# Moving on-chip tiles by multiples of 64 bytes against each other in an attention, dense and LoRA-SwiGLU kernel

## The reference

```python
x = x + attention(x, ...)      # 32 query heads, 8 key/value heads of 128, 512 cached keys + 128 new ones, RMS norm, rotation
x = x + (x @ W.T + b + (x @ sign(mask[b])) * coeff[b])
x = x + down(silu(gate(x)) * up(x))      # width 1376; gate, up and down each with a LoRA of rank 16, chosen per sequence
x = x + x @ weight[adapter_id[b]].T
```

## Time and profile before

| | us |
|---|---|
| three runs | 1366.54, 1367.86, 1368.14; median 1367.86 |
| the profiled execution, its time | 1367.71 |
| its span, first to last instruction | 1365.6 |
| TensorE busy | 1347.4 (99%) |
| VectorE busy | 1040.9 (76%) |
| ScalarE busy | 840.0 (62%) |
| GpSimd busy | 714.9 (52%) |

### The profile page before, as it was taken

One profiled execution on the slowest core, in us unless ns is written; L12 is line 12 of the kernel. 1 busy time (PEld: TensorE's weight loads), 2 busy tenths in 40 slices (PEclk: granted clock), 3 DMA queues, 4 the chain that ended last, 5 costly groups with the idle time before them and its releaser, 6 DMA issues. The chain is left out here.

```text
span 1365.6 us, 24886 instructions
## 1 busy us (share of the span) xinstructions
PE 1347.4 (99%) x7810; PEld 1189.8 (87%) x7810; DVE 1040.9 (76%) x2122; ACT 840.0 (62%) x2212; POOL 714.9 (52%) x970
## 2 busy tenths in 40 slices
PE   8999999999999999999999999999999989999998
PEld 7898898888889888899888889888888868888886
DVE  7888777877787778777877787778777877748547
ACT  7666665666566666665666666566655774545444
POOL 7766465546555655555555555564545633413204
PEclk9999999999999999999999999999999999999999
DMA  5355225522552264136414631573210453355432
GB/s 198 97 178 166 63 80 168 151 66 77 188 128 53 79 205 130 31 108 200 108 31 134 203 77 31 154 208 99 63 31 17 139 173 124 123 185 163 164 124 84
DMA packets 161994, 163.91 MB, mean 120 GB/s; under 512 B 121488, under 2 KB 129296, under 8 KB 151568
## 3 DMA queue, kind: packets, MB, share of 16 engines
q1 hardware_dynamic: 156144, 128.06, 32.2%
q0 software_dynamic: 5792, 35.13, 7.9%
HBM read 131.71 MB, written 31.46 MB: 119 GB/s over the span
## 5 line engine op out<-in xcount | busy, mean ns | idle before, releaser
L444 POOL TENSOR_SCALAR at_probs<-at_probs,at_row_inv 128x640 f32<-128x640 f32 x256 | 211.1, 825 | 152.4 <-DVE at_row_inv L808 152.4
L540 ACT ACTIVATE at_pT_hi<-ps 128x512 fp32r<-128x512 f32 x320 | 186.6, 604 | 99.5 <-PE ps L65 51.2
L802 DVE CUSTOM_DVE_ANT_0 at_scores<-ps,at_mask,at_inv_rms 128x640 f32<-128x640 f32 x256 | 220.1, 878 | 31.7 <-PE ps L65 31.4
L585 ACT ACTIVATE at_probs<-at_scores,at_neg_max 128x640 f32<-128x640 f32 x256 | 211.9, 836 | 48.2 <-DVE at_neg_max L802 48.1
L750 DVE TENSOR_TENSOR at_pT_lo<-ps,at_pT_hi 128x512 fp32r<-128x512 f32 x320 | 212.7, 686 | 26.1 <-ACT at_pT_hi L540 21.4
L63 PE MATMUL ps<-ds_hi,x_hi 128*128 128x512 f32 (+1 forms) x564 | 193.6, 343 | 4.7 <-POOL ds_lo L1194 2.0
L65 PE MATMUL ps<-ds_hi,x_lo 128*128 128x512 f32 (+1 forms) x564 | 192.1, 341 | 0.0
L580 ACT ACTIVATE at_square<-ps 128x128 bf16<-128x128 f32 x256 | 67.2, 277 | 172.2 <-DVE a_raw L781 172.2
L1022 PE MATMUL ps<-ident,at_probs 128*128 128x128 f32 x1280 | 160.6, 273 | 1.6 <-POOL at_probs L444 1.6
L63 PE MATMUL ps<-at_kT_hi,ds_lo 128*128 128x320 f32 x512 | 158.0, 309 | 1.4 <-DVE at_neg_max L802 0.8
L65 PE MATMUL ps<-at_kT_hi,ds_lo 128*128 128x320 f32 x512 | 158.1, 309 | 0.0
(11 more groups left out here) (206 smaller groups left out, 3429.4 us busy)
## 6 DMA issues: line engine op xcount, KB each, us to landing
kT_pages<-shared SPq DMA_DIRECT2D x14, 1024.0 KB
v_pages<-shared SPq DMA_DIRECT2D x14, 1024.0 KB
kv_raw<-kT_pages SPq DMA_DIRECT2D x56, 256.0 KB, 3.9
kv_raw<-v_pages SPq DMA_DIRECT2D x56, 256.0 KB, 4.2
sw_wgu_raw<-in_sw_gu SPq DMA_DIRECT2D x22, 512.0 KB, 3.4
staging<-in_L_cond_Wq SPq DMA_DIRECT2D x8, 1024.0 KB, 6.9
staging<-in_L_cond_Wo SPq DMA_DIRECT2D x8, 1024.0 KB, 4.8
shared<-in_mask_Bx4096x_ik SPq DMA_DIRECT2D x7, 1024.0 KB, 5.4
```

The source lines that it names most:

```text
L444: pool.tensor_scalar(probs[:, h, :], probs[:, h, :], row_inv[:, h:h + 1], 1.0, ALU.mult, ALU.mult).then_inc(probs_done, 1)
L540: act.activation(out, src, ACT.Copy).then_inc(done, 1)
L585: act.activation(probs[:, h, :], scores[h % 2][:], ACT.Exp, bias=neg_max[:, h:h + 1], scale=-1.0, accum_out=row_sum[:, h:h + 1]).then_inc( ...
L802: dve.tensor_tensor_reduce(out=scores[h % 2][:], in0=slot(h), in1=mask[:, b, :], scale=inv_rms[b % 2][:, h:h + 1], scalar=3.0e38, op0=ALU. ...
```

## The change

No instruction is added or taken away. The order in which tiles are created is changed, and with it their addresses; `ints` and `floats` are cut to the columns that are used, and the pads go or change size. The same rule of placing gives, within 512 bytes:

- `x_hi`, `x_lo`, `ds_hi0`, `ds_lo0`, `ds_lo1`, `kT`, `probs`, `q_rot`, `wgu`, `wd`, `ad_cols`, `t_rows`, `b_rows`, `a_cols` at 0;
- `ds_hi1` and `kv_raw` at 192; `v` and `oT` at 192; `pT` and `woT` at 256; `acts` at 64; `ident` stays at 128.

```diff
-        square = sb("square", [P, G + 1, D], BF16)
-        warm = sb("warm", [P, 2, G])
-        neg_max = sb("neg_max", [P, G])
...
-        woT_hi = sb("woT_hi", [P, G, DM], F32R)
-        woT_lo = sb("woT_lo", [P, G, DM], F32R)
...
-        v_hi = [sb(f"v_hi{j}", [P, KC, D], F32R) for j in range(2)]
-        v_lo = [sb(f"v_lo{j}", [P, KC, D], F32R) for j in range(2)]
...
         probs = sb("probs", [P, G, KEYS])
+        ints_sb = sb("ints", [P, 2 * B + 1], I32)
+        sumsq = [sb(f"sumsq{j}", [P, G + 1]) for j in range(2)]
+        d_eps = sb("d_eps", [P, G])
+        v_hi = [sb(f"v_hi{j}", [P, KC, D], F32R) for j in range(2)]
+        v_lo = [sb(f"v_lo{j}", [P, KC, D], F32R) for j in range(2)]
+        oT_hi = sb("oT_hi", [P, G * S], F32R)
+        oT_lo = sb("oT_lo", [P, G * S], F32R)
+        minus_half = sb("minus_half", [P, G])
+        row_sum = sb("row_sum", [P, G])
         pT_hi = [sb(f"pT_hi{j}", [P, G * S], F32R) for j in range(3)]
         pT_lo = [sb(f"pT_lo{j}", [P, G * S], F32R) for j in range(3)]
+        woT_hi = sb("woT_hi", [P, G, DM], F32R)
+        woT_lo = sb("woT_lo", [P, G, DM], F32R)
         RING = len(pT_hi)
-        oT_hi = sb("oT_hi", [P, G * S], F32R)
-        oT_lo = sb("oT_lo", [P, G * S], F32R)
+        square = sb("square", [P, G + 1, D], BF16)
+        warm = sb("warm", [P, 2, G])
+        neg_max = sb("neg_max", [P, G])
...
-        self.x_hi = ctx.enter_context(nc.sbuf_tensor("x_hi", [P, DC, B * S], F32R))
-        self.x_lo = ctx.enter_context(nc.sbuf_tensor("x_lo", [P, DC, B * S], F32R))
-        hi0 = ctx.enter_context(nc.sbuf_tensor("ds_hi0", [P, DC, DM], F32R))
-        self.lo = [ctx.enter_context(nc.sbuf_tensor(f"ds_lo{j}", [P, DC, DM], F32R)) for j in range(2)]
-        self.coeff2, self.minus_coeff, self.sign_bias = (
-            ctx.enter_context(nc.sbuf_tensor(name, [P, LINE_STEP // 3], F32))[:, 0:B] for name in ("ds_coeff2", "ds_minus_coeff", "ds_sign_bias"))
-        self.hi = [hi0, ctx.enter_context(nc.sbuf_tensor("ds_hi1", [P, DC, DM], F32R))]
+        self.coeff2 = ctx.enter_context(nc.sbuf_tensor("ds_coeff2", [P, B], F32))
+        self.minus_coeff = ctx.enter_context(nc.sbuf_tensor("ds_minus_coeff", [P, B], F32))
+        hi1 = ctx.enter_context(nc.sbuf_tensor("ds_hi1", [P, DC, DM], F32R))
         self.masks.append(ctx.enter_context(nc.sbuf_tensor("kv_raw", [P, DC * DM], F32)))
         self.bias_sb = ctx.enter_context(nc.sbuf_tensor("ds_bias", [P, DM], F32))
         self.a_raw = ctx.enter_context(nc.sbuf_tensor("a_raw", [P, DM], F32))
+        self.sign_bias = ctx.enter_context(nc.sbuf_tensor("ds_sign_bias", [P, LINE - LINE_STEP], F32))[:, 0:B]
+        self.x_hi = ctx.enter_context(nc.sbuf_tensor("x_hi", [P, DC, B * S], F32R))
+        self.x_lo = ctx.enter_context(nc.sbuf_tensor("x_lo", [P, DC, B * S], F32R))
+        self.hi = [ctx.enter_context(nc.sbuf_tensor("ds_hi0", [P, DC, DM], F32R)), hi1]
+        self.lo = [ctx.enter_context(nc.sbuf_tensor(f"ds_lo{j}", [P, DC, DM], F32R)) for j in range(2)]
...
+        a_cols = sb("a_cols", [P, PAIRS, 2 * DC, 2, 4, RANK], F32R)
+        sel = sb("sel", [P, 2])
+        t_sel, b_sel = sel[:, 0:1], sel[:, 1:2]
+        warm = sb("warm", [P, 1])
         acts_hi = [sb(f"acts_hi{j}", [P, NTOK], F32R) for j in range(2)]
         acts_lo = [sb(f"acts_lo{j}", [P, NTOK], F32R) for j in range(2)]
-        ctx.enter_context(nc.sbuf_tensor("sw_line", [P, LINE - LINE_STEP], F32))
-        a_cols = sb("a_cols", [P, PAIRS, 2 * DC, 2, 4, RANK], F32R)
+        ad_raw = [sb("ad_raw0", [P, QUAD, FC, RANK]),
+                  shared[2][:, PAIRS * DM:PAIRS * DM + QUAD * FC * RANK].rearrange("p (q c r) -> p q c r", q=QUAD, c=FC)]
```

More of the change, by code:

```diff
@@ L153, in attention @@
         probs = sb("probs", [P, G, KEYS])
+        ints_sb = sb("ints", [P, 2 * B + 1], I32)
[7 more added lines that the diff above has]
+        row_sum = sb("row_sum", [P, G])
         pT_hi = [sb(f"pT_hi{j}", [P, G * S], F32R) for j in range(3)]
         pT_lo = [sb(f"pT_lo{j}", [P, G * S], F32R) for j in range(3)]
+        woT_hi = sb("woT_hi", [P, G, DM], F32R)
+        woT_lo = sb("woT_lo", [P, G, DM], F32R)
         RING = len(pT_hi)
-        oT_hi = sb("oT_hi", [P, G * S], F32R)
-        oT_lo = sb("oT_lo", [P, G * S], F32R)
+        square = sb("square", [P, G + 1, D], BF16)
+        warm = sb("warm", [P, 2, G])
+        neg_max = sb("neg_max", [P, G])
         kv_stage = shared[0]
-        sumsq = [sb(f"sumsq{j}", [P, G + 1]) for j in range(2)]
-        d_eps = sb("d_eps", [P, G])
-        minus_half = sb("minus_half", [P, G])
         inv_rms = [sb(f"inv_rms{j}", [P, G + 1]) for j in range(2)]
-        row_sum = sb("row_sum", [P, G])
         row_inv = sb("row_inv", [P, G])
@@ L167, in attention @@
         page_idx = sb("page_idx", [P, 1], U32)
-        ints_sb = sb("ints", [P, 4 * B], I32)
-        floats_sb = sb("floats", [P, 3 * D])
+        floats_sb = sb("floats", [P, 2 * D + D // 2 + 2 + B])
         key_idx = sb("key_idx", [P, B], U32)
@@ L1255, in swiglu_buffers @@
         "b_raw": [sb(f"b_raw{j}", [P, PAIRS, 2, P]) for j in range(3)],
-        "ad_raw": [sb("ad_raw0", [P, QUAD, FC, RANK]),
-                   shared[2][:, PAIRS * DM:PAIRS * DM + QUAD * FC * RANK].rearrange("p (q c r) -> p q c r", q=QUAD, c=FC)],
         "bd_raw": shared[2][:, 0:PAIRS * DM].rearrange("p (q d) -> p q d", q=PAIRS),
-        "sel": sb("sel", [P, 2]),
         "w_loaded": [sem(f"w_loaded{j}") for j in range(3)],
@@ L1319, in dense_swiglu @@
         GATE, UP, DOWN, TD, SIDE = 0, 1, 2, 6, 7
-        wgu_raw, wd_raw, b_raw, ad_raw, bd_raw, sel = (early[n] for n in ("wgu_raw", "wd_raw", "b_raw", "ad_raw", "bd_raw", "sel"))
+        wgu_raw, wd_raw, b_raw, bd_raw = (early[n] for n in ("wgu_raw", "wd_raw", "b_raw", "bd_raw"))
         w_loaded, b_loaded, ad_loaded, bd_loaded, sel_loaded = (
@@ L1325, in dense_swiglu @@
         x2_done = dense.x2_done
-        t_sel, b_sel = sel[:, 0:1], sel[:, 1:2]
         x_hi, x_lo = ([t[:, :, h * NTOK:(h + 1) * NTOK] for h in range(2)] for t in (dense.x_hi, dense.x_lo))
-        warm = sb("warm", [P, 1])
         wgu_hi = sb("wgu_hi", [P, 2, 2 * DC * P], F32R)
@@ L1340, in dense_swiglu @@
         acts = [shared[0][:, j * NTOK:(j + 1) * NTOK] for j in range(2)]
+        a_cols = sb("a_cols", [P, PAIRS, 2 * DC, 2, 4, RANK], F32R)
+        sel = sb("sel", [P, 2])
+        t_sel, b_sel = sel[:, 0:1], sel[:, 1:2]
+        warm = sb("warm", [P, 1])
         acts_hi = [sb(f"acts_hi{j}", [P, NTOK], F32R) for j in range(2)]
         acts_lo = [sb(f"acts_lo{j}", [P, NTOK], F32R) for j in range(2)]
-        ctx.enter_context(nc.sbuf_tensor("sw_line", [P, LINE - LINE_STEP], F32))
-        a_cols = sb("a_cols", [P, PAIRS, 2 * DC, 2, 4, RANK], F32R)
+        ad_raw = [sb("ad_raw0", [P, QUAD, FC, RANK]),
+                  shared[2][:, PAIRS * DM:PAIRS * DM + QUAD * FC * RANK].rearrange("p (q c r) -> p q c r", q=QUAD, c=FC)]
+        early["ad_raw"] = ad_raw
         w3_hi, w3_lo = dense.hi, dense.lo
```

## The result

The changed kernel takes 1371.06 us in the median (1369.82 to 1374.28, 20 runs) beside 1368.57 for the kernel before (1366.54 to 1371.49, 20 runs): ratio 1.0019, 95% interval 1.0012 to 1.0026. It is slower beyond the noise, by just under the 0.2% that was called the least a measurement can tell. Forecast were 1357 us and a range of 1349 to 1371; the time lies a few hundredths above the range and on the other side of no change. The profiled execution took 1369.82 us, with a span of 1368.0, 2.4 more than before.

The account below looks back on a forecast made before the run. TensorE, busy for 1347.4 of 1365.6 us, was taken to bound the kernel through its step per matmul. From 1367.7, terms of -5.6, -5.0 and +0.2 us gave 1357.3, rounded to 1357 us, range 1349 to 1371.

Parts of the forecast that it names:

- the cover of 0.6 us: Last normalising ends 0.6 us before the next transposes start; forecast to last, as a pass shortens at most 0.2 us.
- rival A: All matmuls: addresses don't matter, uneven steps come from changes of width and kind; 1367 to 1368 us, chance 0.17.
- second term of part (1): Output, values, down: 64 bytes apart lowers overhead per matmul by 2.5 ns over 1992 matmuls, -5.0 us.
- The first term: Output, values, down: groups settle earlier to the level step of 0.2267 us; -5.6 us, bounds 0 and -8.4.
- Rival B: Matmuls over v, oT, wd: 64 bytes above is a bad distance, +6.4 us, groups behind +0.6; 1374 to 1375, chance 0.15.
- Part (2): Tokens, query weights, queries, kT move from 128 to 0, staying level: 0 us, allowing 1.5 either way if place counts.
- (3): a_cols, stationary under the tokens in 64 matmuls of 256 columns, becomes level: +0.2 us.

Follow-up runs that it names:

- e2: Changed kernel with pT and woT 64 bytes below v and oT, and acts 64 below wd: 1370.66 us, ratio 1.0019.
- e6: Kernel before with woT alone moved to 64 bytes above oT: 1369.06 us, ratio 1.0007.
- e14: Kernel before with ds_hi1, the weights of new keys and values, at 128, level with the tokens: 1367.78 us, ratio 0.9999.
- e12: Changed kernel with large tiles at 0, but oT and woT at 192 with the keys' and values' weights: 1368.11 us, ratio 1.0001.
- e10: Changed kernel with oT at 0 and woT at 64, still 64 bytes apart: 1369.1 us, one run.
- e11: Changed kernel with v and oT at 0, and pT and woT at 64: 1368.82 us, ratio 1.0008.
- e4: Changed kernel with pT and woT 192 bytes above v and oT, and acts 192 above wd: 1370.81 us, one run.
- e8: Kernel before with pT, woT and acts 32 bytes above what they meet: 1371.99 us, one run.
- e13: Changed kernel with v at 192, pT at 384, oT and woT level at 192, acts level with wd: 1367.87 us, ratio 0.9998.
- e1: Changed kernel with v, oT, pT and woT all at 192 and acts at 0 like wd: 1369.21 us, ratio 1.0012.
- e9: Kernel before with oT and woT both at 320, level with the keys' and values' weights: 1367.57 us, ratio 0.9999.
- e7: Kernel before with pT alone moved to 64 bytes above v: 1368.54 us, one run.
- e5: Changed kernel with every large matmul tile at 0, only ds_hi1 at 192: 1369.35 us, ratio 1.0006.

## Why the prediction was wrong

**What was right.** TensorE sets the time alone; no other engine comes up behind it; the cover of 0.6 us was not touched; the time depends on addresses, not on the widths alone (rival A as a mechanism falls with e2, e6 and e14, though its time came nearer). The Trainium skill ("TensorE: Matmul & The Clock Gate", "Step-by-step: what each phase is for") says that loading the next tile's weights takes no read bandwidth from the running matmul. No run here separates the load from the stream, so none shows that sentence wrong by its letter; but with every shape and order unchanged, output goes from 229.3 (e12) to 233.6 ns with the addresses of the two tiles, which the sentence gives no reason to expect. No change, which the prediction worked out from it, is what was measured to within 0.2%.

**The step that failed is the second term of part (1),** the -5.0 us. It took the 10.8 ns overhead of the keys' and values' row, at 192 bytes and 256 columns, for 512 columns at 64 bytes. The runs put in its place: settled overhead of 512 columns is 13.3 ns level; 20.0 at 64 above in the changed kernel's output, 15.6 at the same distance after another neighbour (e6, e10, e11, and half of the changed kernel's own down groups); 19.0 at 128; 20.0 at 192 or 64 below, and at 32. None is under level. The term was +6.7 ns for output instead of -2.5, and measured against the present unsettled step, +2.8 ns, 2.15 us. Over all three groups the two terms together, forecast at -10.6 us, came out at +3.6. The row itself was a poor witness: its distance does make it cheap for 256 columns (e14), but it runs at 10.8 or 7.4 ns of overhead at one distance (e2, e4, e8, e13), depending on what runs ahead.

**The first term,** -5.6 us for settling earlier, had the right kind and the wrong yield. The output of the changed kernel does settle: its second gap is within 1 ns of the last but one. It settles at 233.3, so the excess over 226.7 went from 4.1 to 6.9 ns instead of away. For down the prediction took the step of the earlier trace rows for all 22 groups; only the eight behind transposes run so, and all 22 together had 0.7 us to give, not 1.0. Where a group was given an easier entry at level distance (e1, e9, e12), it gave 1.1 us of the output's 3.2, a third.

**Rival B had the sign and half of the mechanism.** It priced a bad distance at 0.2342 for output, down and values alike, +6.4 us. Output measured 233.6 and the worse half of the down groups 233.3, near that price; the other half of down settles at some 229, and values are at 231.4, with gaps of 226 to 236 in their short groups and not a flat 233. The mean of the three groups over their 1992 matmuls is 232.27, for 230.5 before, just under the 0.2324 us where B said that slower begins. The groups behind, which B put at +0.6, measured +0.6. But 64 bytes above is not bad by itself, as B has it: after another neighbour the same distance is no worse than level unsettled (output 230.4 in e6, values 229.2 in e7). B's reason against, that the earlier trace rows alternate between two distances, was no reason: 20.9 ns there and 20.0 here.

**Part (2) and (3):** place worth nothing, shown by e5 for a shift of 128 bytes (0.2 us for an allowance of 1.5 either way); `a_cols` +0.1 us for +0.2. What (2) left out is that `v` and `oT` move against the tokens and scores around them. The distance from one group's stream to the next group's first stationary tile changed too, and with it the entry: e10, which changes that seam and keeps the 64 bytes, takes 2.4 us off the output, all of the 2.15 that the change had added. The values are of the same kind: from e10 to e11, with `v` made level with its neighbours and the 64 bytes kept, they go from 231.6 to 229.1, and the scores from 145.8 to 146.5, so the changed kernel's -0.6 us in the scores came with `v` and `pT` too. What an uneven seam does inside the engine no run shows.

## What to carry to other kernels

When the matmul engine is full, divide timeline starts by count: the step, not the written length, shows some ns of layout. Keep what streams and what is loaded meanwhile level within 256 bytes unless a run shows better, and include the seam to the next group, since gains in one group came back as losses in another in most layouts here. In fourteen layouts, ten of them cheaper by 1 to 3 us in at least one group, the sum of all gaps moved between -1 and +4.4 us of 1366: this knob is spent, and a cheap row of another width is no price for a group.

## What the runs showed of the hardware

With 128 by 128 stationary tiles of 4-byte numbers at 2.4 GHz granted, the gap between two matmul starts is the columns' time and an overhead that depends on the distance of the moving tile from the stationary tile loaded meanwhile, with a period of 256 bytes as far as tried (e2 and e4 settle alike to 0.1 ns, 128 and 64 do not repeat the level gap; the second half of `kT` lies 256 bytes further than the first, and all scores settle at 146.7), and on history. A run of equal matmuls falls into a fixed gap or a cycle of two to seven. The output's settled gaps repeat to 1.5 ns in 58 or more of the 64 passes, while the queries of the kernel before go in two ways in turn, 2.72 and 2.74 us. In those passes the overheads round every cycle read here sum to a whole multiple of 6.67 ns, which is the time of 16 columns, 64 bytes of the moving stream: 13.3; 20.0; 18.3 + 12.5 + 15.8 = 46.6; 22.5 + 17.5 = 40.0; 133.4 over seven; for 256 columns 13.3, 6.7, or three that sum to 33.3. It takes up to ten matmuls to get there. What takes turns at that pace the traces do not say; it stays open.
